# Cross-attention with tokens on partitions, its keys and values made in the first stage's tail, and spectral products in parts

## What is computed

```
x = layernorm(x + attn(x))            # correlation by FFT, top-k, softmax
x = layernorm(x + xattn(x, context))  # 64 context tokens per batch entry
x = layernorm(x + ffn(x))             # a self-attention and a mixture of 8 experts

# attn: Q, K, V = x W + b;  corr = irfft(rfft(Q) * conj(rfft(K)))  over the 1024 tokens
# w = softmax(top_k(corr));  out = w V[first 16 tokens];  out @ Wo + bo

# xattn:
q = x @ Wq.T + bq                     # 4 x 1024 x 256
k, v = split(context @ Wkv.T + bkv)   # 4 x 64 x 256 each
att = softmax(q k^T / 4) per head     # 16 heads, 64 keys
y = att v;  return y @ Wo.T + bo
```

## Time and profile before

| | us |
|---|---|
| median of 3 runs | 1738.43 (1734.7 to 1738.7) |
| the profiled execution's own time | 1739.07 |
| its span, first to last instruction | 1736.9 |
| first stage | 0 to 185.45 |
| cross-attention | 185.45 to 431.2 |
| its first scores | at 225.5 |
| later stages | 431.2 to 1736.9 |

### The profile page before, as it was taken

How to read it: one execution, slowest core, us unless ns; L and a number is a source line. 1 busy time by engine, 2 the same in 40 slices (tenths; PEclk the granted TensorE clock), 3 DMA queues, 4 the chain that set the end, 5 groups by cost and what they waited for, 6 DMA issues and landing times. The chain is left out here.

```text
span 1736.9 us, 35640 instructions
## 1 busy us (share of the span) xinstructions
PE 1593.7 (92%) x11156; PEld 910.5 (52%) x11157; DVE 1138.7 (66%) x1701; ACT 845.8 (49%) x1505; POOL 382.0 (22%) x662
## 2 busy tenths in 40 slices
PE   6998689987886999999999999999998939999997
PEld 3554346654453344444444444444435839888886
DVE  2545379998654888888888888888883742223322
ACT  1211144442442577777777777777775302221221
POOL 3110211110432111111111111111110114555554
PEclk9999599998998899999999999999998959999999
DMA  6000200000233111111111111111102935655552
GB/s 200 0 0 1 64 1 1 0 1 1 91 127 100 28 36 32 35 37 32 32 37 35 32 35 37 33 32 37 36 20 53 316 120 187 195 181 187 198 182 75
DMA packets 82275, 123.69 MB, mean 71 GB/s; under 512 B 24339, under 2 KB 48533, under 8 KB 82230
## 3 DMA queue, kind: packets, MB, share of 16 engines
q1 hardware_dynamic: 76614, 107.77, 20.3%
q0 software_dynamic: 5616, 15.34, 2.6%
HBM read 96.56 MB, written 26.08 MB: 71 GB/s over the span
## 5 line engine op out<-in xcount | busy, mean ns | idle before, releaser
L1240 DVE TENSOR_REDUCE sb_m_mx<-banks 128x1 f32<-128x1024 f32 x512 | 603.3, 1220 | 103.2 <-PE banks L1113 102.6
L1206 ACT ACTIVATE sb_m_pT<-banks 128x512 f32<-128x512 f32 x1024 | 552.3, 593 | 158.9 <-PE banks L1139 150.5
L1139 PE MATMUL banks<-sb_m_q,sb_m_k 99*128 99x512 bf16 x1024 | 329.4, 383 | 1.4 <-ACT sb_m_pT L1206 1.3
L1113 PE MATMUL banks<-sb_m_k,sb_m_q 96*128 96x512 bf16 x1024 | 293.3, 388 | 12.9 <-DMA sb_m_k<-k_parts 10.4
L1153 PE MATMUL banks<-sb_m_pT,sb_m_v 128*32 128x256 f32 x4096 | 274.9, 386 | 0.7 <-ACT sb_m_pT L1206 0.7
L1153 PEld LDWEIGHTS banks<-sb_m_pT,sb_m_v 128*32 128x32 f32 x4096 | 107.0, 109 | 152.6 <-issue 74.7
L1139 PEld LDWEIGHTS banks<-sb_m_q,sb_m_k 99*128 99x128 bf16 x1024 | 99.1, 97 | 162.0 <-ACT sb_m_pT L1206 84.4
L1113 PEld LDWEIGHTS banks<-sb_m_k,sb_m_q 96*128 96x128 bf16 x1024 | 98.9, 98 | 125.2 <-issue 14.8
L1772 ACT ACTIVATE sb_e_hT<-banks 128x512 f32<-128x512 f32 x78 | 46.6, 597 | 239.0 <-PE banks L1731 231.9
L1084 POOL CAST sb_m_mx_parts<-sb_m_mxT 8x128 bf16<-8x128 f32 x64 | 18.3, 285 | 629.4 <-ACT sb_m_mxT L1219 608.1
L1742 PE MATMUL banks<-w,sb_e_hT 128*128 x624 | 143.9, 384 | 8.5 <-ACT sb_e_hT L1772 4.1
(11 more groups left out here) (215 smaller groups left out, 1835.9 us busy)
## 6 DMA issues: line engine op xcount, KB each, us to landing
w<-in_w SPq DMA_DIRECT2D x47, 1024.0 KB, 9.0
sb_m_q<-q_parts SPq DMA_DIRECT2D x384, 32.0 KB, 1.7
sb_m_k<-k_parts SPq DMA_DIRECT2D x384, 32.0 KB, 1.8
q_parts<-sb_c_parts SPq DMA_DIRECT2D x24, 256.0 KB, 2.2
k_parts<-sb_c_parts SPq DMA_DIRECT2D x24, 256.0 KB, 2.2
X<-in_x SPq DMA_DIRECT2D x4, 1024.0 KB, 11.0
x_rows<-X SPq DMA_DIRECT2D x8, 512.0 KB, 9.5
z_rows<-sb_g_zs SPq DMA_DIRECT2D x8, 512.0 KB, 5.1
```

The costliest lines, as they stand in the source:

```text
L1113: mm = pe.matmul(ps[2 * (k % 2) + h][:, :], q_s[0:R, i, k * P:(k + 1) * P], k_s[0:R, i, h * 512:(h + 1) * 512], start=True, stop=True)
L1139: pe.matmul(ps[rotating(use)][:, :], k_s[:, i2, m * P:(m + 1) * P], q_s[:, i2, h * 512:(h + 1) * 512], start=True, stop=True).then_inc(sco ...
L1206: act.activation(pT[:, m, h * 512:(h + 1) * 512], ps[rotating(f"b{m}{h}")][:, :], ACT.Exp).then_inc(exped, 1)
L1240: dve.tensor_reduce(mx[:, par % 2, k:k + 1], pz[:, 2 * (k % 2):2 * (k % 2) + 2, :].rearrange("p q n -> p (q n)"), AX.X, ALU.max).then_inc( ...
```

## The change

**First stage, spectral products in parts.** The eight products come in the order 2, 3, 6, 7, 0, 4, 1, 5. The cross spectrum is made in three chunks, as soon as 4, 6 and 8 of them are copied. PE transforms the even part back first (it needs the first chunk only), then the odd part. In the last entry the six maxima come ahead of the cross products, and each of the last two follows its own row.

```diff
+    SEQ = (2, 3, 6, 7, 0, 4, 1, 5)
+    CHUNKS = ((2, 4, 4), (0, 1, 6), (1, 2, 8))
-                pe.wait_ge(cross_done, b + 2)
-                for c in range(KT):
-                        pe.matmul(ps[4 + 2 * c][:, :], cross[:, f, cs], inv_odd[:, n, :], ...)
+                pe.wait_ge(cross_done, 1 + 3 * b + 1)
+                ...        even part of both c, then
+                pe.wait_ge(cross_done, 1 + 3 * b + 3)
+                ...        odd part of both c
+                if last:
+                    dve.wait_ge(corr_done, 2 + G - KT)
+                    largest(0, G - KT)
+                for lo, hi, ready in CHUNKS:
+                    dve.wait_ge(qk_copied, 8 * b + ready)
+                    ...    the same six operations on parts lo to hi
-                    largest(0, G - KT)
```

```diff
+            for c in range(KT):
+                for k in range(KT):
+                    mm = pe.matmul(ps[c][:, 0:B * C], w_kv[:, k, c * P:(c + 1) * P], ctxT[:, k, :], ...)
+            for n, b in enumerate((2, 3, 0, 1)):
+                for k in range(KT):
+                    for half in range(2):
+                        pe.matmul(ps[b][C * half:C * half + C, 0:P], ctxT[:, k, b * C:(b + 1) * C],
+                                  of_half(w_kv[:, k, D:2 * D], half), start=(k == 0), stop=False)
+                for half in range(2):
+                    mm = pe.matmul(ps[b][C * half:C * half + C, 0:P], ones_row[:, :], of_half(bias_v[:, :], half), ...)
```

```diff
-                        mm = pe.matmul(ps[2 * (r % 2) + c][:, :], qT[:, c, ...], kblk[:, c, ds(b, 1), :], ...)
+                    for half in range(2):
+                        rows = slice(64 * half, 64 * half + 64)
+                        mm = pe.matmul(ps[2 * (n % 2) + half][:, c * 256:(c + 1) * 256], qT[rows, c, g % 2, r * P:(r + 1) * P],
+                                       kblk[rows, c, b, :], start=True, stop=True, skip_group_check=True)
+            def turn_result(n):
+                pe.wait_ge(y_done, n + 1)
+                for k in range(KT):
+                    tr = pe.transpose(ps[6][:, k * P:(k + 1) * P], y[:, n % 2, k * P:(k + 1) * P], ident[:, :])
+            def products(n):
+                pe.wait_ge(probsT_copied, n + 1)
+                need(pe, yT_copied, n)
+                for j in range(HP):
+                    mm = pe.matmul(ps[6][:, jj * VW:(jj + 1) * VW], prT[:, n % 2, j, :], vx[:, n // TPB, jj, :], ...)
-                    dve.reciprocal(rec[:, :], ps[6][:, D:2 * D]).then_inc(rec_done, 1)
+                    dve.reciprocal(rec[:, :, :], both[:, :, 2 * DK:VW]).then_inc(rec_done, 1)     # 128x16
```

More of the change, by code:

```diff
@@ L498, in need @@
+    SLOTS = NT + 3
+    CLOSES = 4
     def need(eng, signal, value):
-        if not isinstance(value, int) or value > 0:
+        if value > 0:
             eng.wait_ge(signal, value)
-    def over_slots(eng, slot):
-        for r in range(TPB):
-            slot(0, r)
-        with eng.Fori(1, B - 1) as b:
-            for r in range(TPB):
-                slot(b, r)
-        for r in range(TPB):
-            slot(B - 1, r)
-        for r in range(3):
-            slot(B, r)
-    def tile(b, r, lag):
-        n = b * TPB + r - lag
-        return n if not isinstance(n, int) or 0 <= n < NT else None
@@ L574, in _, with power @@
[L574 to L582 removed]
+            def power(G):
+                pool.wait_ge(var_done, G + 1)
+                pool.tensor_tensor(rstd[:, G % 2, :], mv[:, G % 2, :, 1], neg_half[:, 0:GT], ALU.pow).then_inc(rstd_done, 1)
@@ L599, in _, with piece @@
-            pe.wait_ge(k_copied, KT)
-            pe.wait_ge(vblk_done, 2 * B)
-            def make(number, kind, g, parity, part):
-                need(pe, piece_copied, number)
-                if kind == 1:
-                    pe.wait_ge(xs_done, g + 1)
+            def piece(p, bank):
+                G, part = p // 4, p % 2
+                if p % 4 < 2:
+                    pe.wait_ge(xs_done, GT * G + 2 * part + 2)
+                    if part == 0 and G > 0:
+                        pe.wait_ge(piece_copied, p)
@@ new lines, in _ @@
+            for p in range(4):
+                piece(p, ps[4 + p])
+            for n in range(SLOTS):
+                if n < NT:
+                    score(n)
+                if 0 <= n - 2 < NT:
+                    turn_result(n - 2)
+                if 0 <= n - 1 < NT:
+                    turn_weights(n - 1)
+                p = 4 + n if 4 + n < 4 * NG else None
+                if p is not None:
+                    need(pe, res_done, n - 2)
+                    need(pe, piece_copied, p if n else 0)
+                    piece(p, ps[7])
+                if 0 <= n - 1 < NT:
+                    products(n - 1)
+                if 0 <= n - 2 < NT:
+                    project(n - 2, p)
@@ new lines, in tile_stats, with moments_of @@
+            def tile_stats(m):
+                dve.bn_stats(stats[:, m % GT, :], X[:, m, :]).then_inc(stat_done, 1)
+            def moments_of(G):
+                dve.wait_ge(stat_done, GT * (G + 1))
+                alone(dve, spare)
+                for r in range(GT):
+                    last = dve.bn_aggr(mv[:, G % 2, r, :], stats[:, r, :])
+                last.then_inc(aggr_done, 1)
+                dve.wait_ge(aggr_done, G + 1)
+                dve.tensor_scalar(mv[:, G % 2, :, 1], mv[:, G % 2, :, 1], EPS, None, ALU.add).then_inc(var_done, 1)
```

518 lines of the change are left out of this document (253 added, 265 removed).

## The result

The kernel with the change takes 1730.36 us, the median of 7 runs (1725.95 to 1732.1), against 1738.43, the median of 7 runs of the kernel before: a ratio of 0.9952, with a 95% interval of 0.9938 to 0.9966. It is faster by 8 us, where 35 were forecast.

The account below looks back on a forecast made before the run. The prediction took the loop as bound by PE, with DVE right behind. Gains 25.0 before the loop, -3.4 loop, 6.8 after it and 7.4 tail sum to 35.8, taking 1739.1 to 1703 us; range 1690 to 1732.

Parts of the forecast that it names:

- the rival of row halves without overlap: Loop scores: the two row halves don't run side by side, price 27.5 us, total 1730.5; chance 0.14.
- the main case: Whole kernel: the summed gains and losses give 1703 us, own range 1692 to 1716; chance 0.77.
- Before the loop: Second stage up to the first scores: load waits, keys, values and key spreading removed, 15 us left of 40.05, gain 25.
- First stage's tail: End of first stage: products in parts bring the count to 169.6, product L236 1 us less; gain 7.4, 4 to 9.
- Products: Loop, PE: 16 instructions with weights 128 wide and 34 columns take 1.71 per slot, dearer by 0.70 per tile.
- that rival (1663): Loop products cost by their columns, sixteen 0.45 and not 1.71, 40 us less, total 1663; chance 0.02.
- The new wait: Loop: products wait for ACT's copy, 1.4 after the transposes; about 0.9 us of PE idle with a transposing piece.
- Scores: Loop, PE: 8 instructions of 256 columns in two row halves overlap fully, 0.86 in place of 1.72.
- the 0.10 for the change of shape: Loop scores: 0.10 us allowed for a change of instruction shape on either side, read from L644's 0.96.
- The clock falls in the loop: Rival: PE streams less, each 3.4 us low-clock stretch costs 1.7; slower from 24 stretches, 1757 at one per slot; chance 0.07.
- From the last maximum on: End of the second stage, last maximum to stage change: 11.9 us in place of 18.7, gain 6.8.
- DVE, ACT and the reciprocal: Loop: reciprocal falls from 1.75 to about 0.2, DVE about 4.4 of 6.2 us, ACT 0.4 more; neither ends last.

Follow-up runs that it names:

- The last two kernels: Count moved ahead of the last two batch entries' values, against the kernels with weight transposes first and either wide or old products: 1709.49 and 1708.68 us.
- the edit that covers it: Against the changed kernel, PE transposes the weights of tile n-1 ahead of the scores, and ACT copies them first: 1716.94 us, ratio 0.9868.
- the smallest one: The kernel before with only the first stage's spectral products in parts; keys, values and loop as before: 1729.49 us, ratio 0.9938.

## Why the prediction was wrong in size

The direction was right, the gain was 8 of 35 us by the medians. The range held by luck: it reached up to 1732 only to take in the rival of row halves without overlap, which the traces refute, and the main case's own range, 1692 to 1716, was missed. The signs by which the prediction was to know itself wrong didn't show either: the distances' mean is 6.81 (the limit was 7), the loop's clock 0.94 (0.9). What failed is one term put at nothing, the falls of the clock in the loop, and one mis-sized, the changes of shape around the row halves. Point by point:

- **Before the loop**, gain 25.0 forecast to the first scores: the stage takes 13.5 to them (192.70 less 179.2) in place of 15, a gain of 26.5. Right.
- **First stage's tail**, 7.4 forecast, 6.3 measured. The parts did what was said: without keys and values the count was to go at 166.5 and went at 166.17. With them it was to go at 169.6 and went at 169.84, but that match is luck. The transforms ended at 164.22 and not at 162.9, since the early fall of the clock had cost some 1.5, and keys and values then took 5.6 and not 6.7. Without such a fall the count goes at 168.2 to 168.5. Wrong was the "1 more" for the product at a warmer clock: it took 5.41, as before, since PE still stood idle for 2.41 ahead of it. The last two kernels show what that clock is worth, and how to get it.
- **Products**, 1.71 forecast, 1.70 measured; with 64 columns 1.73. The pace doesn't follow the columns that stream; 8, 34 and 64 of them cost nearly the same. The Trainium skill (TensorE: Matmul & The Clock Gate, "LDWEIGHTS") gives a load's time as its columns over 1.2 GHz, by which 107 ns is an estimate for 128 columns; the trace agrees, with 106 ns per product. What the prediction made of the Trainium skill's other rule (TensorEngine Tiling, "Instruction Overhead"), that sixteen would be nearly free, is not borne out, and that rival (1663) is out.
- **The new wait**, forecast in slots without a projection piece, was there and only there. From the weight transposes to the products it takes 1.28 in transposing slots, where 1.4 was taken (idle 0.68 for 0.9), and more in the last slots, with no piece (1.11 idle). The mechanism was right, and the edit that covers it took 0.44 off the transposing slots.
- **Scores**: full overlap was right, and the rival without it (1730.5) is wrong, although the time came out where it said. The matching number shows nothing: the scores are in 1.06.
- **The term that was mis-sized** is the 0.10 for the change of shape. It was read rightly from the projection's 0.96 in the kernel before. Three of those four instructions take 0.22, and the last, next to products of another shape, stands 0.31 ahead of them (296.24 in the earlier trace rows):

```profile
295.93 0.38 PE L644 MATMUL banks<-sb_b_w_o,sb_b_yT 128*128 128x256 f32 x1
```

  But this prices one border, and the way to the row halves and back costs 0.34. Another 0.08 had no term at all: the projection's first instruction takes that much longer behind the new products, with row halves or without (the 0.95 of the kernel with scores over all rows, against 0.86). Of the 0.28 that every slot is over, the changes of shape are 0.24 and the projection's start 0.08, less 0.05 at the weight transposes. Over 30 slots that is 8.4 us; the other 1.8 of the slots' 10.2 are not taken apart here.
- **The term that was missing** is the clock. "The clock falls in the loop" stood only as a rival, told as slower than before and as deciding from 24 stretches on; with fewer it was in no sum. There were 27.2 us of it in the loop, which cost 13.6 by half their length and 11.5 by the kernel with wide products, which takes them away and changes little else. It is the largest error of the sum. The argument against it was that the idle time is under half as long as at the old loop's end and DVE doesn't bind. Neither counted: the falls came with 0.68 of idle ahead of the products and with DVE waiting. (The idle time at the old loop's end is 1.25 and 2.25 us in turn, not over 2 before each projection.) A mechanism with a price per occurrence ought to have stood in the main sum with some count between none and 24, and the range's centre with it.
- **From the last maximum on**, 11.9 forecast (its terms add up to 11.8), 14.7 measured. The timeline of the end shows why: the exponential is ready at 408.50, but the transposes that want it stand in PE's queue behind the products and projection of the tile before and start at 410.29 (1.8), and the last projection runs at a low clock (from 415.0 for 3.4). With the transposes first and wide products the same stretch takes 12.2 (391.29 to 403.47).
- **DVE, ACT and the reciprocal** were right: 0.26 for the reciprocal where 0.2 was taken, 0.39 for ACT's new copy, and neither engine ends last.

What stays open: the places of the falls are known for one execution per kernel only, and the profiled execution of after is 4.4 us below the median of its seven runs. The mean granted clock is on record for every execution, and fits falls whose number differs from run to run: over the seven runs of after it goes from 0.960 in the fastest to 0.953 in the slowest. The four of the kernel with wide products have 0.962 to 0.966, all above those seven, so its better clock isn't an accident of one trace. The four with the transposes first have 0.955 to 0.960, which overlaps the seven; that their gain lies partly in the loop's clock rests on its one trace. Also not tried was a change with keys and values where they were, and the rest new.

## What to carry to other kernels

On PE, columns streamed are not only a cost: a loop that trades wide instructions for narrow ones that wait for their weights, and has a short wait in it, can lose its clock with PE 93% busy, so price such a change with falls of the clock in the main sum. The cure can be free, either unread columns under the weight load or an order of the queue in which the wait has cover. And try the parts of a large change singly: here the smallest one carried all the gain, and a one-instruction move in the queue gave 3 us more. Last, a time or a count that matches the forecast shows little until its terms have been held against the trace one by one: three matches here, the range, the rival's 1730.5 and the count's 169.6, were luck.

## What the runs showed of the hardware beyond that

- Sixteen float32 products with weights 128 wide take 1.70 us with 34 columns and 1.73 with 64: thirty more columns cost 0.002 us per instruction.
- Two row halves of 64 work side by side in full (eight instructions of 256 columns in 1.06, of which 0.2 is the change of shape; 1.73 over all rows; a pair in the middle takes 0.22, as one instruction over all rows does), and one pair of changes between whole and half rows costs 0.34 us.
- With 34 columns and 0.68 of idle every other slot the clock fell to 1.2 GHz for 27.2 of 211 us; with 64 columns and the same idle for none of 199; with 34 columns and 0.13 of idle for none between 208 and 382 us; with products of 128 columns and up to 1.1 of idle in nearly every slot for none between 206 and 363 us. Each is one trace.
- A product of sixteen instructions of 256 columns takes 5.41 us after 2.41 of idle, with a fall of the clock at its start, and 3.72 after 0.51, without one.
